# A sparse-attention layer's setup: two of four chunks done in pieces inside the loop, query scratch laid out by tile

## The chip, the cores and the metric

One core of one Trainium2 chip. The metric is the device time of one execution in microseconds, the median of several. The kernel is a whole stack of eight layers in fp32 (some products split into two rounded halves), written with explicit queues and semaphores.

## The reference

`x` is 2048 tokens of 128 features. Eight layers follow each other, each `x = x + layer(norm(x))`: gated linear attention, a four-product FFN, a state-space layer, the same FFN, the top-k attention, an integer FFN, linear attention, the integer FFN. The change is in the top-k attention. Cut to what matters:

```python
c_kv = x @ W_dkv                                  # 32 latents a token
q_i = (x @ idx_wq).reshape(B, L, 4, 64); k_i = x @ idx_wk
I = einsum('bths,h->bts', relu(einsum('bthd,bsd->bths', q_i, k_i)), idx_w)
I = where(local, inf, I); I = where(causal, -inf, I)   # window of 64, causal
_, idx = top_k(I, 96)                             # 64 of the window, 32 picked
c_q = x @ W_dq                                    # 64
query_c = c_q @ W_uq; query_r = pope(c_q @ W_qr, angles_q)   # softplus, rotated
key_r = pope((x @ W_kr)[idx], angles_k)           # rotated by rank of the pick
scores = (query_c . (c_kv @ W_uk)[idx] + query_r . key_r) * scale
out = softmax(scores) @ (c_kv @ W_uv)[idx] @ W_out
```

The kernel merges W_uq with W_uk and W_uv with W_out, so a key is one row of 96 numbers (64 for the rotary part, 32 latents) in a table in DRAM.

## The kernel before

Tokens lie along the free axis, in 4 chunks of 512 or 16 tiles of 128. A tile has 8 groups of 16 queries, 128 groups in all. PSUM has 8 banks of 512 columns.

**Setup (`topk_setup`, one version for each engine), before any attention.** When the fourth layer is done, SP loads four weights and all rope tables. PE merges the weights by 32 small matmuls (four banks, copied out by ACT at L1228 to L1230). Then for each of 4 chunks: `front` (latent query, keys, rotary queries; softplus as Abs, Exp, Ln on ACT, max and add on DVE at L1652 to L1656), `index` and `back` (four index queries and one index key, each rounded by ACT at L1250 and its rest kept by DVE at L1669; latent queries; keys turned into rows). DVE rotates the queries for the window (`rotate`, L1678 to L1680), POOL those for the picks (L558 to L560). SP stores queries, latents and key rows in DRAM. Tiles 0 and 1 are scored and picked in this stage (`EARLY = 2`).

**The loop (`topk`).** It is unrolled over slots, the same for all engines; slot s has attention step n = s - ATTN_LAG, here s - 7. Each engine has a fixed order in a slot:

- PE: `rows_turn(n+1)` (L891), `scores(n)`, `values(n-2)`, the scores of index units in `SLOT_STEPS[s]`, `probs_turn(n-1)` (L911, L912), and at a tile's end `out_project`, and `index_turn`.
- ACT: `rows_copy(n+1)` (L1303), `probs_norm(n-1)` (L1314), `out_copy(n-2)` (L1329), queries regrouped, rectified index scores (L1286), `probs_copy(n-1)`, `probs(n)` (L1309).
- DVE: `rows_rotate(n+2)` (L1748), `sum_invert(n-1)` (L1766), the addition to x, mask and picks (L1725, L1727, L1729) that come first, `row_max(n)` (L1758), then sums (L1713, L1716) and the other picks. A pick round finds 8 maxima, their places, and drops them, each over all columns of the tile; four rounds. The "rows" step (L1737) puts the finished list where POOL reads it.
- POOL: `gather(i)`: 32 indirect DMAs a tile (16 for tile 0), 4 a group, into one of two buffers. It waits for the list of tile i, and for each group for `values` of the same group of tile i-2.
- SP: for each tile 10 loads of queries (four rotary parts and one latent part, for window and picks) and 8 of values, one a group.

`SLOT_STEPS` spreads sums and picks of tiles 2 to 15 over slots 0 to 117 in proportion to a cost (columns plus 60); the list of a tile is ready a slot after its "turn". So the last, tile 15, is in slot 118. The attention of tile i covers slots 8i+7 to 8i+14.

## Time and profile before

| | us |
|---|---|
| median of 3 runs | 1364.27 |
| lowest, highest | 1357.66, 1373.55 |
| profiled execution, its span | 1540.3 |
| before the top-k setup | 450 |
| setup | 127 |
| loop | 807 |
| three layers behind | 156 |

The profiled execution has no time of its own beside its span from the first to the last instruction. In the views, a group of instructions is named by line, engine, operation and tiles; many helpers share a line (L579 is every matmul made by `mm`). PE's durations are modelled, some of its records can be missing, and "remote" or "issue" as the end of a wait means that no recorded event was found for it.

### The profile page before, as it was taken

The numbers are of one execution on the slowest core, as the hardware profiler recorded it, in microseconds if no ns is written. First come the engines' busy times: TensorE is split into PE (matmuls) and PEld (weight loads), VectorE is DVE, ScalarE is ACT, GpSimd is POOL, SyncE is SP. The second block draws the span as 40 slices with busy tenths as digits, with TensorE's granted clock in tenths as the row PEclk, the third lists the DMA queues.
The fourth block names the chain that finished last, engine by engine and source line by source line (L and its number), as shares of the span: only waits on it lengthen the run. The fifth ranks groups of instructions, "written<-read, shape, count | busy, mean of one in ns | idle before, by whom it ended". The sixth has DMA issues, their size and how long they took to land. (4 is left out here: it accounts for less than half of the span.)

```text
span 1540.3 us, 20077 instructions
## 1 busy us (share of the span) xinstructions
PE 1138.3 (74%) x6808; PEld 807.1 (52%) x6808; DVE 835.0 (54%) x1764; ACT 737.4 (48%) x1795; POOL 532.3 (35%) x532
## 2 busy tenths in 40 slices
PE   6499989979996782777677866777667636388996
PEld 2288756726671221555555645565555525375554
DVE  3477555345534564765565565665666635125436
ACT  3822367718755441554444444454545524265325
POOL 2000000000002386466666666666766463400000
PEclk7699899959985665766666677666767756577889
DMA  5000000000022143133223221322212222100000
GB/s 187 1 1 1 1 1 0 1 0 1 0 74 91 64 126 71 43 56 54 51 39 55 55 58 33 57 55 55 56 35 57 44 52 48 27 15 14 1 1 28
DMA packets 74488, 61.99 MB, mean 40 GB/s; under 512 B 31570, under 2 KB 59028, under 8 KB 73876
## 3 DMA queue, kind: packets, MB, share of 16 engines
q1 hardware_dynamic: 58516, 36.31, 9.7%
q0 software_dynamic: 15872, 24.41, 7.6%
q8 instruction: 55, 0.90, 0.2%
q14 instruction: 45, 0.37, 0.1%
HBM read 52.53 MB, written 8.13 MB: 39 GB/s over the span
## 5 line engine op out<-in xcount | busy, mean ns | idle before, releaser
L545 POOL DMA_INDIRECT arena_lo<-key_table,idx_T x496 | 490.9, 990 | 302.0 <-issue 133.9
L579 PE MATMUL bank<-arena_lo 128*32 128x32 f32 (+6 forms) x1656 | 209.8, 276 | 112.1 <-issue 55.0
L579 PEld LDWEIGHTS bank<-arena_lo 128*32 128x32 f32 (+5 forms) x1656 | 178.0, 166 | 165.7 <-issue 128.6
L558 POOL TENSOR_TENSOR arena_lo<-arena_lo 128x512 f32<-128x512 f32 x8 | 11.8, 1474 | 474.2 <-DVE arena_lo L1656 473.9
L1303 ACT ACTIVATE arena_hi<-bank 96x512 f32<-96x512 f32 x128 | 74.7, 584 | 120.3 <-remote 71.7
L1329 ACT ACTIVATE arena_hi<-bank 32x128 f32<-32x128 f32 x128 | 33.6, 262 | 200.3 <-remote 166.3
L891 PE MATMUL bank<-ident,arena_hi 128*96 128x128 f32 x512 | 111.2, 359 | 22.8 <-DVE arena_hi L1748 22.8
L1716 DVE SCALAR_TENSOR_TENSOR arena_lo<-arena_lo,iw 128x512 f32<-128x512 f32 (+4 forms) x114 | 76.0, 667 | 84.5 <-ACT arena_lo L1286 54.3
L579 PE MATMUL bank<-index_k_hi,index_q 128*128 128x512 f32 (+5 forms) x160 | 92.0, 576 | 21.0 <-ACT arena_lo L1286 11.4
L1286 ACT ACTIVATE arena_lo<-bank 128x512 f32<-128x512 f32 (+4 forms) x152 | 76.0, 510 | 56.3 <-remote 26.6
L911 PE MATMUL bank<-ident,arena_hi 128*128 128x128 f32 x128 | 48.8, 381 | 65.9 <-ACT arena_hi L1314 50.5
L891 PEld LDWEIGHTS bank<-ident,arena_hi 128*96 128x96 f32 x512 | 80.6, 168 | 31.1 <-DVE arena_hi L1748 24.2
L1758 DVE CUSTOM_DVE_ANT_0 arena_hi<-bank,score_mask 128x208 f32<-128x208 f32 x124 | 46.4, 374 | 90.2 <-issue 60.8
L579 PE MATMUL bank<-arena_hi,arena_lo 32*128 32x128 f32 x256 | 57.6, 411 | 49.2 <-ACT arena_hi L1329 48.1
L579 PEld LDWEIGHTS bank<-arena_hi,arena_lo 32*128 32x128 f32 x256 | 53.0, 311 | 54.1 <-ACT arena_hi L1329 50.8
L1725 DVE MAX8 arena_lo<-arena_lo 128x8 f32<-128x320 f32 (+13 forms) x56 | 75.6, 1350 | 0.7
L579 PE MATMUL bank<-index_k_lo,index_q 128*128 128x512 f32 (+5 forms) x160 | 75.9, 476 | 0.0
L1727 DVE FIND_INDEX8 idx_u<-arena_lo 128x8 uint32<-128x320 f32 (+13 forms) x56 | 75.7, 1351 | 0.0
L911 PEld LDWEIGHTS bank<-ident,arena_hi 128*128 128x128 f32 x128 | 22.3, 175 | 92.8 <-ACT arena_hi L1314 66.9
L579 PE MATMUL bank<-arena_hi 96*32 96x128 f32 x1024 | 70.9, 361 | 0.0
L1748 DVE TENSOR_TENSOR arena_hi<-arena_lo,rank_rope 128x384 f32<-128x384 f32 x128 | 70.7, 552 | 0.3 <-issue 0.3
L1314 ACT ACTIVATE arena_hi<-arena_hi 128x208 f32<-128x208 f32 x128 | 59.1, 462 | 13.6 <-DVE arena_hi L1766 5.9
(257 smaller groups left out, 2463.0 us busy)
## 6 DMA issues: line engine op xcount, KB each, us to landing
arena_lo<-key_table,idx_T POOLq DMA_INDIRECT x496
arena_lo<-q_l SPq DMA_DIRECT2D x64, 64.0 KB
arena_lo<-q_lat SPq DMA_DIRECT2D x32, 128.0 KB
arena_lo<-q_g SPq DMA_DIRECT2D x64, 64.0 KB
h<-in_h SPq DMA_DIRECT2D x2, 1024.0 KB, 7.8
q_l<-arena_hi SPq DMA_DIRECT2D x8, 256.0 KB
q_g<-arena_hi SPq DMA_DIRECT2D x8, 256.0 KB
q_lat<-arena_hi SPq DMA_DIRECT2D x8, 256.0 KB
```

Of the source, the lines that this page charges most:

```text
L545: pool.indirect_dma_start(out=G[b][:, q, :], out_offset=None, in_=key_table[0:index_width(i), :], in_offset=bass.IndirectOffsetOnAxis(ap=i ...
L579: return pe.matmul(out_, lhsT, rhs, start=start, stop=stop, **kw)
L891: last = pe.transpose(bank[2 + n % 2][0:ROW, j * P:(j + 1) * P], GR[n % 2][:, j, :], ident[:])
L911: pe.transpose(score_bank(n)[:, 0:P], Pr[n % 2][:, 0:P], ident[:])
L1286: fn(relu_[:, u % 4, 0:w], bank[6 + u % 2][:, 0:w], ACT.Relu).then_inc(i_relu, 1)
L1303: fn(GT[n % 2], bank[2 + n % 2][0:ROW, :], ACT.Copy).then_inc(a_gts, 1)
L1314: fn(Pr[n % 2], Pr[n % 2], ACT.Copy, scale=rsum[:, n % 2:n % 2 + 1]).then_inc(a_pn, 1)
L1716: ins = v.scalar_tensor_tensor(s_, r_, iw[:, h:h + 1], s_, ALU.mult, ALU.add)
L1725: steps.did(v.max(best, sc))
L1727: steps.did(v.max_index(idx_u[:, 8 * k:8 * k + 8], best, sc))
L1748: v.tensor_tensor(GR[n % 2], G[i % 2][:, 4 * g:4 * g + 4, :], rank_rope[:].unsqueeze(1).to_broadcast([P, 4, ROW]), ALU.mult).then_inc(a_ro ...
L1758: steps.did(v.tensor_tensor_reduce(out=Sm[b], in0=score_bank(n)[:, 0:KEYS], in1=mask[:], scale=1.0, scalar=LOWEST, op0=ALU.add, op1=ALU.ma ...
```

## The change

- The setup is cut into 12 pieces a chunk (`PIECES`): index key, four index queries, latent query, keys, two rotary queries, rows, two latent queries. A piece is one product of PE (`piece`), a copy of ACT, Exp and Ln for three of them, and an end on DVE (`piece_end`) for eight.
- `topk_front` replaces `topk_setup` and the second half of the norm before it: chunks 0 and 1 with a ring of four banks, between them the norm's steps and the picks of tiles 0 and 1. Chunks 2 and 3 go into the loop: a piece a slot from slot 5 and from slot 30 in banks 3 and 5, and then four slots with a quarter of the query rotation each (`queries_rotate`, three instructions).
- All queries are rotated by DVE; POOL only gathers, and starts when the first chunk's rows are stored.
- The weights are merged before the state layer (`merge_weights`); their loads start when the FFN's weights have been rounded.
- Rotary tables and key tables are loaded by chunk into one buffer each; index queries are kept for two chunks.
- Scratch for queries is laid out by tile, so that a tile's queries are 6 loads with runs of 4 KB on the DRAM side, and its values 2 loads instead of 8.
- ATTN_LAG 7 becomes 4, PICK_SLOTS 118 becomes 115. `rows_turn` uses one bank instead of two; turned lists lie in bank 7 with the odd index units; projected outputs in the score bank of the tile's last group.

```diff
+        q_rot = {n: dram("q_" + n, (NT, DR, NH, P)) for n in ("l", "g")}
+        q_lat = dram("q_lat", (NT, DC, NH, P))
...
+        def window_rows(i, g0, g1):
+            s0 = max(i * P + g0 * GQ - LW, 0)
+            step = GQ * ROW if i * P + g0 * GQ >= LW else 0
+            return bass.AP(key_table.tensor, s0 * ROW + 2 * DR, [[ROW, WIN], [step, g1 - g0], [1, DC]])
...
-        ATTN_LAG = NG - 1
-        PICK_SLOTS = NG * NT - 10
+        ATTN_LAG = 4
+        PICK_SLOTS = NG * NT - 13
...
+        PIECES = ("ik", "iq0", "iq1", "iq2", "iq3", "cq", "raw", "qp0", "qp1", "rows", "ql0", "ql1")
+        NPIECE = len(PIECES)
+        PIECE_SLOT = {2: 5, 3: 30}
+        def piece_bank(c, k):
+            return bank[(NPIECE * c + k) % 4] if c < FRONT else bank[(3, 5)[k % 2]]
...
+        def pieces_at(s):
+            return [(c, s - s0) for c, s0 in PIECE_SLOT.items() if 0 <= s - s0 < NPIECE]
...
+        def turns_at(s):
+            return [(c, s - s0 - NPIECE) for c, s0 in PIECE_SLOT.items() if 0 <= s - s0 - NPIECE < 4]
...
+        start, per_slot = 1, (cost(sum(SUMS[FRONT + 1:] + PICKS[FRONT:], []))) / (PICK_SLOTS - 1)
...
+            sp.wait_ge(f_w, 5)
             for n, dst in (("WuqT", WuqT), ("WukT", WukT), ("WuvT", WuvT), ("Wout", Wout)):
                 sp.dma_start(dst, d[n]).then_inc(t_w, 16)
...
+            def load_tables(c):
+                if c:
+                    sp.wait_ge(t_rot, 4 * c)
                 for k, n in enumerate(("cos_ql", "sin_ql", "cos_qg", "sin_qg")):
...
+                    sp.dma_start(rope_tab[:, k, :], d[n][:, c * C:(c + 1) * C]).then_inc(t_tab[c], 16)
...
+            def load_queries(i):
...
                     sp.wait_ge(a_q, 4 * i)
-                half = DR // 2
                 for dst, n in ((QL_in, "l"), (QG_in, "g")):
-                    for r in range(4):
-                        src = q_rot[n][r % 2][:, i * P:(i + 1) * P].rearrange("(h f) t -> f h t", f=half)
-                        sp.dma_start(dst[r * half:(r + 1) * half], src).then_inc(q_loaded, 16)
-                    src = q_lat[:, i * P:(i + 1) * P].rearrange("(h c) t -> c h t", c=DC)
-                    sp.dma_start(dst[2 * DR:ROW], src).then_inc(q_loaded, 16)
+                    for r in range(2):
+                        sp.dma_start(dst[r * DR:(r + 1) * DR], q_rot[n][i]).then_inc(q_loaded, 16)
+                    sp.dma_start(dst[2 * DR:ROW], q_lat[i]).then_inc(q_loaded, 16)
...
+            def load_values(i):
...
                 if i >= 2:
                     sp.wait_ge(a_pv, NG * (i - 1))
-                for g in range(NG):
-                    s0 = max(i * P + g * GQ - LW, 0)
-                    sp.dma_start(Vloc[b][:, g, :], key_table[s0:s0 + WIN, 2 * DR:ROW]).then_inc(v_loaded[b], 16)
+                for g0, g1 in ((0, LW // GQ), (LW // GQ, NG)):
+                    sp.dma_start(Vloc[b][:, g0:g1, :], window_rows(i, g0, g1)).then_inc(v_loaded[b], 16)
...
+            load_key_rope(1)
+            store_queries(0, 0)
+            store_queries(0, 1)
+            store_latents(0)
+            load_tables(1)
+            load_queries(0)
+            load_values(0)
...
+            for s in range(SLOTS):
+                for c, k in pieces_at(s - 1):
+                    if PIECES[k] == "rows":
+                        store_rows(c)
+                    elif PIECES[k] == "ql1":
+                        store_latents(c)
+                    elif PIECES[k] == "qp0" and c + 1 < NCH:
+                        load_key_rope(c + 1)
+                for c, half in turns_at(s - 1):
+                    if half % 2 == 1:
+                        store_queries(c, half // 2)
+                    if half == 3 and c + 1 < NCH:
+                        load_tables(c + 1)
+                i, at_ = divmod(s - ATTN_LAG, NG)
+                if at_ == 0 and 0 <= i < NT - 1:
+                    load_queries(i + 1)
+                if at_ == 2 and 1 <= i < NT - 1:
+                    load_values(i + 1)
...
-            pool.wait_ge(x_ready, 4 * L_TOPK + 4)
-            for c in range(NCH):
-                pool.wait_ge(t_mu, c + 2)
-                pool.wait_ge(t_tab[c], 80)
-                pool.wait_ge(t_store_g, STORES_Q * (c + 1))
-                cos, sin = rope_tab[c][:, 2, :], rope_tab[c][:, 3, :]
-                for b, (f0, f1, op) in enumerate(((cos, sin, ALU.subtract), (sin, cos, ALU.add))):
-                    steps.did(pool.tensor_tensor(rot_tg[:, 0, :], mu[c % 2][:, 0, :], f0, ALU.mult))
-                    steps.did(pool.tensor_tensor(rot_tg[:, 1, :], mu[c % 2][:, 1, :], f1, ALU.mult))
-                    last = pool.tensor_tensor(rot[:, 2 + b, :], rot_tg[:, 0, :], rot_tg[:, 1, :], op)
...
+            for i in range(NT):
+                if i % 4 == 0:
+                    pool.wait_ge(t_store_k, STORES_K * (i * P // C + 1))
                 gather(i)
...
@@ -771,6 +855,7 @@
             def ssm():
                 pe.wait_ge(s_ssm, N_SSM)
+                merge_weights()
                 with pe.Fori(0, NCH) as c:
...
                 for h in range(NH):
-                    last = mm(bank[0][0:DCQ, h * DC:(h + 1) * DC], WuqT[:, h, :], WukT[:, h, :])
+                    last = mm(bank[4][0:DCQ, h * DC:(h + 1) * DC], WuqT[:, h, :], WukT[:, h, :])
                 for h in range(NH):
-                    last = mm(bank[1 + h // 4][0:DC, (h % 4) * P:(h % 4 + 1) * P], WuvT[:, h, :], Wout[:, h, :])
+                    last = mm(bank[2 + h // 4][0:DC, (h % 4) * P:(h % 4 + 1) * P], WuvT[:, h, :], Wout[:, h, :])
                 last.then_inc(t_wm, 1)
...
+            def piece(c, k):
+                name, o_, tokens = PIECES[k], piece_bank(c, k), xn[:, c * C:(c + 1) * C]
+                if c < FRONT:
+                    if NPIECE * c + k >= 4:
+                        bank_released(*divmod(NPIECE * c + k - 4, NPIECE))
+                elif k >= 2:
+                    bank_released(c, k - 2)
+                elif c > FRONT:
+                    bank_released(c - 1, NPIECE - 2 + k)
...
+            def topk_front():
+                pe.wait_ge(s_tk, N_TK)
+                pe.wait_ge(x_ready, 4 * L_TOPK + 4)
+                ln_center(L_TOPK, 1)
+                for k in range(4):
+                    piece(0, k)
+                ln_mean(L_TOPK, 1)
+                for k in range(4, 7):
+                    piece(0, k)
+                ln_spread(L_TOPK, 1)
+                pe.wait_ge(ln_applied, LN0 + 4 * L_TOPK + 4)
+                sums(0)
+                for k in range(7, 10):
+                    piece(0, k)
+                index_turn(0)
+                sums(1)
+                for k in range(10, NPIECE):
+                    piece(0, k)
+                for k in range(5):
+                    piece(1, k)
+                index_turn(1)
+                for k in range(5, NPIECE):
+                    piece(1, k)
...
             def rows_turn(n):
                 pe.wait_ge(a_rot, n + 1)
-                if n >= 2:
-                    pe.wait_ge(a_gts, n - 1)
+                if n >= 1:
+                    pe.wait_ge(a_gts, n)
                 for j in range(4):
-                    last = pe.transpose(bank[2 + n % 2][0:ROW, j * P:(j + 1) * P], GR[n % 2][:, j, :], ident[:])
+                    last = pe.transpose(bank[2][0:ROW, j * P:(j + 1) * P], GR[n % 2][:, j, :], ident[:])
                 last.then_inc(a_gt, 1)
...
+                if n % (4 * NG) == 0:
+                    pe.wait_ge(t_kl, i * P // C + 1)
                 if n >= 3:
                     pe.wait_ge(a_otc, n - 2)
+                    if (n - 3) % NG == NG - 1:
+                        pe.wait_ge(a_x, (n - 3) // NG + 1)
...
-                bank5_free((a_x, i + 1))
                 for h in range(NH):
-                    last = mm(bank[5][:, 128:256], Muv[:, h, :], OT[i % 2][:, h, :], h == 0, h == NH - 1,
+                    last = mm(score_bank(NG * i + NG - 1)[:, 3 * P:4 * P], Muv[:, h, :], OT[i % 2][:, h, :], h == 0, h == NH - 1,
...
                             index_scores(i, k)
+                    for c, k in pieces_at(s):
+                        piece(c, k)
                     if 0 <= n - 1 < GROUPS:
                         probs_turn(n - 1)
                     if 0 <= n - 2 < GROUPS and (n - 2) % NG == NG - 1:
...
+            def piece_exp(c, k):
+                if softplus_of(c, k):
+                    a = softplus_of(c, k)[0]
+                    steps.did(fn(a, a, ACT.Exp, scale=-1.0))
...
+            def piece_log(c, k):
+                if softplus_of(c, k):
+                    a = softplus_of(c, k)[0]
+                    n = a.shape[0]
+                    fn(a, a, ACT.Ln, bias=one_col[0:n]).then_inc(t_ln, 1)
...
+            def topk_front():
+                ln_square(L_TOPK, 1)
+                for k in range(4):
+                    piece(0, k)
+                ln_sqrt(L_TOPK, 1)
+                act.preload_act_table_set("natural_log_exp_and_others")
+                for k in range(4, 7):
+                    whole_piece(0, k)
+                sums(0)
+                for k in range(7, 10):
+                    whole_piece(0, k)
+                sums(1)
+                for k in range(10, NPIECE):
+                    whole_piece(0, k)
+                for k in range(NPIECE):
+                    whole_piece(1, k)
...
-                fn(GT[n % 2], bank[2 + n % 2][0:ROW, :], ACT.Copy).then_inc(a_gts, 1)
+                fn(GT[n % 2], bank[2][0:ROW, :], ACT.Copy).then_inc(a_gts, 1)
...
+                    for c, k in pieces_at(s):
+                        piece(c, k)
                     if 0 <= n - 1 < GROUPS:
                         probs_copy(n - 1)
+                    for c, k in pieces_at(s):
+                        piece_exp(c, k)
                     if 0 <= n < GROUPS:
                         probs(n)
+                    for c, k in pieces_at(s):
+                        piece_log(c, k)
+                act.wait_ge(t_store_l, STORES_L * NCH)
+                steps.leave(steps.k, 1)
...
+            def piece_end(c, k):
+                name, o_ = PIECES[k], piece_bank(c, k)
+                at_, ring = slice(c * C, (c + 1) * C), slice(c % 2 * C, c % 2 * C + C)
+                if name == "ik":
+                    dve.wait_ge(t_iqh, 5 * c + k + 1)
+                    v.tensor_tensor(k_lo[:, at_], o_, k_hi[:, at_], ALU.subtract).then_inc(t_iqs, 1)
+                elif name[:2] == "iq":
+                    q = q_split[int(name[2])][64:P, ring]
+                    dve.wait_ge(t_iqh, 5 * c + k + 1)
+                    v.tensor_tensor(q, o_[64:P, :], q, ALU.subtract).then_inc(t_iqs, 1)
+                elif name == "raw":
+                    dve.wait_ge(t_ln, 3 * c + 1)
+                    v.scalar_tensor_tensor(raw[0:2 * DR, :], o_[0:2 * DR, :], 0.0, raw[0:2 * DR, :], ALU.max, ALU.add)\
+                        .then_inc(t_rawd, 1)
...
+            def queries_rotate(c, half):
+                which, b = divmod(half, 2)
+                cos, sin = rope_tab[:, 2 * which, :], rope_tab[:, 2 * which + 1, :]
+                f0, f1, op = ((cos, sin, ALU.subtract), (sin, cos, ALU.add))[b]
+                if half == 0:
+                    dve.wait_ge(t_mu, 2 * c + 2)
+                    dve.wait_ge(t_tab[c], 64)
+                if c == 0 and half == 0:
+                    dve.wait_ge(ln_inv, 4 * L_TOPK + 4)
+                if c >= 1 and b == 0:
+                    dve.wait_ge((t_store_q, t_store_g)[which], STORES_Q * c)
+                v.tensor_tensor(rot_tmp[:, 0, :], mu[:, 0, :], f0, ALU.mult)
+                steps.did(v.tensor_tensor(rot_tmp[:, 1, :], mu[:, 1, :], f1, ALU.mult))
+                v.tensor_tensor(rot[:, half, :], rot_tmp[:, 0, :], rot_tmp[:, 1, :], op).then_inc(t_rot, 1)
+                dve.wait_ge(t_rot, 4 * c + half + 1)
+            def topk_front():
...
+                for k in range(2):
+                    piece_end(0, k)
+                ln_invert(L_TOPK, 1)
+                for k in range(2, 5):
+                    piece_end(0, k)
+                ln_apply(L_TOPK, 1)
+                piece_end(0, 6)
+                for step, _ in SUMS[0] + PICKS[0][:-1]:
+                    pick(*step)
+                piece_end(0, 7)
+                pick(0, "rows", 0)
+                keys_rotate(0)
+                piece_end(0, 8)
+                for step, _ in SUMS[1] + PICKS[1][:-1]:
+                    pick(*step)
+                for half in range(2):
+                    queries_rotate(0, half)
+                for k in range(4):
+                    piece_end(1, k)
+                pick(1, "rows", 0)
+                for half in range(2, 4):
+                    queries_rotate(0, half)
+                for k in range(4, 7):
+                    piece_end(1, k)
+                keys_rotate(1)
+                for k in (7, 8):
+                    piece_end(1, k)
+                for half in range(4):
+                    queries_rotate(1, half)
...
+                    for c, k in piece_ends_at(s):
+                        piece_end(c, k)
+                        if PIECES[k] == "qp0":
+                            keys_rotate(c)
+                    for c, half in turns_at(s):
+                        queries_rotate(c, half)
```

## Rows read from the trace of the kernel before

**Rows 1.** Windows by stage: start:end, length, busy (instructions) by engine, clock, DMA share, GB/s.

```profile
450.00:577.00 127.00, 91.90 (x194) 36.37 (x194) 68.03 (x124) 57.44 (x90) 56.38 (x47) 0.61 0.36 106
577.00:616.00 39.00, 8.06 (x33) 4.54 (x31) 15.75 (x41) 7.13 (x17) 24.41 (x26) 0.59 0.35 74
616.00:1292.00 676.00, 471.87 (x3466) 366.23 (x3464) 417.33 (x977) 322.50 (x1028) 413.01 (x416) 0.67 0.25 49
1292.00:1384.00 92.00, 54.35 (x504) 46.22 (x504) 19.11 (x85) 36.67 (x133) 30.59 (x32) 0.65 0.13 28
1384.00:1540.30 156.30, 130.09 (x456) 77.78 (x454) 75.27 (x133) 68.49 (x128) 0.00 (x0) 0.86 0.04 14
```

**Rows 2.** POOL's gathers: group of instructions, one line's instructions, timeline.

```profile
L545 POOL DMA_INDIRECT arena_lo<-key_table,idx_T x496 | 490.9, 990 | 302.0 <-issue 133.9 <-remote 71.2 <-PE bank L579 59.1
...
L545 POOL DMA_INDIRECT arena_lo<-key_table,idx_T x496: 942/947/1475, 539.1 to 1334.8; - x166
...
1292.11 0.95 POOL L545 DMA_INDIRECT arena_lo<-key_table,idx_T  x1 [18.55 <-DVE idx_T L1737]
```

**Rows 3.** Timeline of ACT behind the last picks: start, duration, engine, line, operation.

```profile
1369.17 0.58 ACT L1303 ACTIVATE arena_hi<-bank 96x512 f32<-96x512 f32 x1
1371.42 0.59 ACT L1303 ACTIVATE arena_hi<-bank 96x512 f32<-96x512 f32 x1
```

**Rows 4.** Groups of instructions, 616 to 1292: busy, mean ns, idle before them.

```profile
L1725 DVE MAX8 arena_lo<-arena_lo 128x8 f32<-128x576 f32 (+12 forms) x50 | 72.4, 1448 | 0.6
L1716 DVE SCALAR_TENSOR_TENSOR arena_lo<-arena_lo,iw 128x512 f32<-128x512 f32 (+4 forms) x107 | 71.5, 668 | 80.5 <-ACT arena_lo L1286 54.3 <-issue 23.7
...
L1758 DVE CUSTOM_DVE_ANT_0 arena_hi<-bank,score_mask 128x208 f32<-128x208 f32 x107 | 40.0, 374 | 72.0 <-issue 60.8 <-remote 6.9 <-DVE idx_u L1727 0.9
...
L911 PEld LDWEIGHTS bank<-ident,arena_hi 128*128 128x128 f32 x110 | 19.5, 178 | 82.3 <-ACT arena_hi L1314 60.7 <-issue 18.2
L1766 DVE RECIPROCAL arena_hi<-arena_hi 128x1 f32<-128x1 f32 x111 | 17.4, 157 | 28.9 <-ACT arena_hi L1309 23.4 <-issue 4.3
```

**Rows 5.** Stalls: ACT's waits (us, count, longest), and the timeline around two.

```profile
ACT arena_hi L1329 <- remote: 166.3, 46, 25.0
...
914.60 0.27 PE L912 MATMUL bank<-ident,arena_hi 128*80 128x128 f32 x1
919.26 0.27 ACT L1329 ACTIVATE arena_hi<-bank 32x128 f32<-32x128 f32 x1 [4.87 <-remote]
...
611.09 0.19 DVE L1737 CAST idx_T<-bank 128x32 uint32<-128x32 f32 x1 [17.88 <-remote]
```

**Rows 6.** Timeline: the weights' 32 products, and the state layer's start.

```profile
458.47 5.46 PE L579 MATMUL bank<-arena_lo 64*64 64x32 f32 x32
...
312.38 1.87 PE L579 MATMUL bank<-xn,sBT 128*64 x2
...
314.75 1.27 DVE L1632 TENSOR_TENSOR_SCAN ssm_state_sb<-ssm_keep,ssm_carry,bank 64x512 f32 x1 [0.34 <-DVE ssm_carry L1627]
```

**Rows 7.** Timeline: the loop's first sum.

```profile
577.70 0.39 DVE L1713 TENSOR_SCALAR arena_lo<-arena_lo,iw 128x320 f32<-128x320 f32 x1 [3.14 <-issue]
```

**Rows 8.** Groups of instructions, 450 to 577.

```profile
L579 PE MATMUL bank<-xn,Wiq 128*128 128x512 f32 x32 | 22.4, 865 | 0.0
...
L1250 ACT ACTIVATE index_q<-bank 128x512 fp32r<-128x512 f32 x16 | 8.4, 584 | 4.4 <-PE bank L579 3.8 <-issue 0.6
...
L1244 ACT ACT_TABLE_LOAD x4 | 5.1, 1283 | 0.1
...
L1725 DVE MAX8 ln_sq<-ln_sq 128x8 f32<-128x96 f32 (+1 forms) x8 | 2.5, 311 | 0.3
```

**Rows 9.** Timeline of DVE's rotations, and a gather of POOL beside them.

```profile
485.67 1.64 DVE L1679 TENSOR_TENSOR arena_lo<-arena_lo 128x512 f32<-128x512 f32 x1
...
548.14 1.15 POOL L545 DMA_INDIRECT arena_lo<-key_table,idx_T  x1 [0.30 <-issue]
548.51 0.69 DVE L1679 TENSOR_TENSOR arena_lo<-arena_lo 128x512 f32<-128x512 f32 x1
```

533 lines of the change are left out of this document (242 added, 291 removed).

## The prediction

> **What bounds the kernel now.** I read the windows by stage first. The span falls into 450 us before the top-k layer, 127 us of setup up to the first step of the big loop, 39 us of lead-in, 676 us of attention beside picks, 92 us of attention after the last picks, and 156 us of tail [rows 1]. The reader should see that no engine is full in the loop: of 676 us PE is busy 472, DVE 417, POOL 413, ACT 323, at a mean granted clock of 0.67, so most of it at the lower level, 1.2 GHz.
>
> Next, who waits for whom. POOL issues one gather each 1.25 us (0.95 of work at the median and 0.30 of issue [rows 2, 9]); four gathers make a group, so POOL needs 5.0 us a group, 40 us a tile, and it waits: gather(i, g) may start only when values(i-2, g) is done. 59.1 us of its waits are put down to PE. Before the 32 gathers of tile 15 it waits 18.55 us for that tile's index list, and then they run from 1292.1 without waiting but once, the last from 1334.8 [rows 2]. The loop ends 48 us after the last of them, since a long stall of this execution had held the attention back; undisturbed, the end of the loop is the list of tile 15, plus 40 us of gathers, plus some 12 for the last one's landing and five slots, which without picks take 2.25 us each [rows 3]. So what sets the end is the moment when DVE has made the last list (slot 118, step n = 111). Before that, a slot is a round trip between four engines in fixed orders: PE waits 82.3 us in 110 slots for the normed probabilities before it turns them (0.75 us a slot), and DVE waits 72.0, 80.5 and 28.9 us for scores, rectified sums and exponents, 181 us in 111 slots or 1.6 us a slot [rows 4].
>
> **The profiled execution against the median.** It took 1540.3 us, the median is 1364.3, 176 us less. ACT's wait for the values at L1329 alone is 166.3 us here [rows 5], in 46 pieces up to 25.0 us. In one of them PE's last recorded work before its gap ends at 914.9 and what its earlier matmuls release starts at 919.3; another holds DVE for 17.88 us before tile 2's list (L1737) [rows 5]. I take these stalls for the difference, so all differences below are added to 1364.3; I can't show it. Checked: 1364.3 - 450 - 127.7 - 20 (lead-in without that stall) - 52 - 156.3 leaves 558 us for 111 slots, 5.0 us a slot.
>
> **Part 1, weights merged earlier: +5 us (4 to 6).** The 32 small matmuls (5.46 us) move from setup to PE's queue between the last norm spread and the state layer's first matmul. There PE starts at 312.38 and the scan follows 0.34 us late at 314.75 [rows 6]: no cover. The scan would start at 312.4 + 5.5 + 1.9 = 319.8, 5.1 us later. Copies on ACT lie in its idle time.
>
> **Part 2, setup for two chunks instead of four: -57 us (-43 to -68).** Before: 450.0 to DVE's first sum at 577.70, 127.7 us [rows 7]. After, by engine from the same rows. PE: a chunk is 5 index projections, keys, latent query, two rotary and two latent queries, eleven products of two passes at 0.865 us or a little more [rows 8], and four turns: 21 us; two chunks 42, the norm about 6, the scores of tiles 0 and 1 about 6: 54 us, the lower bound with 5 us of fill. DVE, which ends last: norm and first splits until 472; tile 0's sums and picks 7 (11 instructions of three kinds like L1725 at 0.31 us [rows 8], the rest sums) to 480; key rotation and two halves of softplus 2; tile 1's sums and picks 7.5 to 491; now all four quarters of chunk 0's rotation, 12 instructions of 0.69, 8.3 us; nine splits and softplus ends of chunk 1, 6.2. That is 505 to 508. Then chunk 1's rotation needs tables that SP loads only after chunk 0's rotation (502) and two waits behind stores: landed at about 512.7. 12 x 0.69 more ends at 521. Upper bound: another 14 us if the one ring of four banks and picks in DVE's order hold PE up.
>
> The rotations of the picked queries move from POOL to DVE. In the trace a rotation on DVE takes 1.64 us while POOL rotates too and 0.69 while POOL issues gathers [rows 9]; I take 0.69 throughout. The Trainium skill (GPSIMD Engine Reference, 1. Specifications) says the two engines share SBUF interfaces and contend where a DVE instruction has two SBUF inputs. If that held for POOL's gathers too, 48 rotations would cost 0.95 us more each, 46 us in all; the row at 548.51 beside a gather speaks against it. POOL's gathers no longer wait for POOL's rotations; gather(0) can start at about 484 instead of 539, but its rows are needed only at step 0, so nothing comes of it.
>
> Of ACT, the table loads of 1.283 us, one for Exp and one for Ln in each of 4 chunks [rows 8], should go, since one set is loaded ahead. ACT isn't last in my sum, so no gain is booked.
>
> **Part 3, lead-in: -1.5 us.** The lag falls from 7 slots to 4, the picks end at slot 115, again step 111. Spread by the kernel's own costs, 36 sums and picks lie in slots 0 to 6 before, and 24 in slots 0 to 3 after. At 320 to 448 columns I take 0.55 and 0.5 us each, between the mean of the front (0.31, 96 and 192 columns [rows 8]) and that of the loop (1.45, over 400 to 1984 columns [rows 4]): 19.7 and 12.2 us. So step 0 comes 7.5 us earlier relative to the loop's start, but the same picks must then be done in the same 111 steps: 7.5 us of DVE work moves there. DVE has 1.6 us of waits a slot; four fifths of it, 6 us, I book (0 to 8).
>
> **Part 4, two chunks in pieces inside the loop: +32 us (0 to 80).** 24 slots get a piece: on PE two passes (1.73 us) between the sums and the turn of the probabilities, on ACT one to three instructions of 0.6, on DVE one or two of 0.69. Eight slots get a quarter of a chunk's rotation, three instructions, 2.1 us of DVE. Behind PE's piece stand probs_turn, ACT's copy, the exponent, and DVE's reciprocal. PE had 0.75 us of wait just there, so 1.0 us of 1.73 stays: 24 us. Six pieces have Exp and Ln (1.2 us) before and after probs: half, 4 us. Rotations against 1.6 us of DVE waits: 0.5 x 8 = 4. From below nothing, if POOL's 5.0 us a group or the round trip hides all; from above all of it in row, 24 x (1.73 + 0.58) + 7.6 + 17 = 80 (0.58 ACT's copy, L1250 [rows 8]). I take 32, nearer to the lower end, since every engine shows idle time [rows 1].
>
> **Part 5, layout and loads: -6 us (-35 to 0).** A tile's queries are 10 loads, 768 KB in 512-byte pieces, and 8 loads of values; now 6 and 2. They are issued four slots ahead, and ACT waits nowhere for them, so the loads as such bring nothing. But the stall at 914.9 lies where such a load is issued. Were 2.5 us of each of 14 tile changes due to it, 35 us would go; I can't see that outside this profile and take 6. The stores write the same bytes.
>
> **Part 6, shared banks: +3 us (0 to 10).** Turned rows have one bank, lists share a bank with odd sums, projected outputs lie in a score bank. Behind PE's new waits stand scores. DVE's add comes while PE turns rows (1 us), so the wait is mostly covered; 0.2 us a tile.
>
> Sum: 5 - 57 - 1.5 + 32 - 6 + 3 = -24.5 us. 1364.3 - 24.5 = 1339.8, so 1340 (the profiled execution: about 1516). Tail and the 52 us after the last list stay.
>
> **Rivals.**
> A, the pieces are hidden: POOL's 5.0 us a group equals the pace of 5.0. If the attention really follows POOL, or fuller engines are granted more clock, part 4 costs nothing: 1308. For it: idle time on all engines, and PE's passes shorten wherever the full clock is granted. Against: POOL waits for values in the trace, not the reverse. 0.20.
> B, slower: the round trip takes each piece at full length at 1.2 GHz. Part 4 is 80, the time 1388. It becomes slower than before when 32 slots cost over 56.5 us, 1.8 us each. For it: PE busy 70% at the low clock and DVE 62% leave little in a slot of 5. 0.15.
> C, the front gains less or ACT changes tables in the loop. Six Exp-Ln pieces with two loads of 1.283 us are 15.4 us; 15 us of waits in the front do the same: 1355. 0.18. The Trainium skill (ScalarE: Activation LUTs, Table sets) says that natural_log_exp_and_others holds both functions, which speaks for no such loads; no row of before shows that set kept, since each Exp and each Ln has its load.
> D, the change doesn't do what it says: too small to count beside C, for the setup is really two chunks shorter.
>
> **How the numbers follow.** The forecast has 0.47, its own range 1325 to 1355. All cases to eight in ten: 1306 to 1380, which leaves out part of B and little of A. A measurement can tell about 1% from no change, here 1350.6 and 1377.9. Faster: 0.40 of the forecast's 0.47 and all of A, 0.60. Same: the forecast's other 0.07 and C's 0.18, 0.25. Slower: B's 0.15.
>
> **What would show it.** The scan about 5 us later; the first sum of the loop about 71 + 5 us after the norm instead of 127.7; 24 slots longer by 1 us; no table load inside the loop; the last list about 24 us earlier, with 52 us from there to the norm in an undisturbed run. I am wrong if DVE or PE in slots 5 to 20 and 30 to 45 takes over 1.8 us more, if POOL waits for nothing (then A), or if new stalls end at q loads.

## The result

The changed kernel took 1300.1 us (median of 4 runs, 1286.6 to 1303.4) against 1361.0 us before: a ratio of 0.9546 with a 95% interval from 0.9502 to 0.9591, 61 us less. The forecast was 1340, the lower end of its range 1306.

The chips that the runs came to are of two kinds: one runs the kernel before in 1351 to 1374 us and the other in 1525 to 1559 us, and the profile of before that the prediction rests on (1540.3 us) is of the other kind than its median (1364.3 us). A second run of the changed kernel on a chip of the first kind gave 0.9486 (0.9419 to 0.9553, 1290.8 us), one on a chip of the second kind 0.9535 (0.9485 to 0.9585, 1484.7 against 1549.5 us). Below, "gapless" chips are the first kind, for POOL's gathers have no gaps there, and "stalling" chips the second. Each chip was used at one time only, so that the difference lies in the chip and not in the occasion is taken for granted, not shown. Unless a chip is named, a number is of the gapless kind.

The windows by stage of the changed kernel (start:end, length, then busy us with the number of instructions of PE, weight loads, DVE, ACT and POOL, granted clock, DMA share, GB/s), which answer to [rows 1]:

```profile
450.00:512.60 62.60, 44.29 (x125) 20.40 (x123) 43.20 (x100) 33.55 (x64) 29.16 (x29) 0.76 0.46 109
512.60:1119.00 606.40, 484.09 (x3953) 376.77 (x3952) 470.48 (x1129) 375.15 (x1184) 461.58 (x468) 0.75 0.30 72
1119.00:1146.00 27.00, 21.85 (x110) 16.14 (x111) 4.57 (x19) 10.61 (x31) 0.07 (x1) 0.50 0.12 41
1146.00:1301.60 155.60, 129.57 (x435) 77.14 (x433) 73.75 (x129) 64.52 (x121) 0.00 (x0) 0.84 0.02 7
```

The setup is 62.6 us long instead of 127, the tail is as before. Now POOL's gathers in the same trace, the group and then the timeline, answering to [rows 2]:

```profile
L648 POOL DMA_INDIRECT gathered_rows<-key_table,idx_T x496 | 490.8, 990 | 592.8 <-DMA key_table<-key_rows 439.4 <-issue 147.5 <-PE bank L663 5.8
```

```profile
474.91 1.09 POOL L648 DMA_INDIRECT gathered_rows<-key_table,idx_T  x1 [439.44 <-DMA key_table<-key_rows]
...
1049.35 0.17 DVE L1891 CAST idx_T<-bank 128x32 uint32<-128x32 f32 x1
...
1077.95 0.94 POOL L648 DMA_INDIRECT gathered_rows<-key_table,idx_T  x1 [0.30 <-issue]
...
1118.13 0.94 POOL L648 DMA_INDIRECT gathered_rows<-key_table,idx_T  x1 [0.30 <-issue]
```

The reader is to see that POOL, over the whole kernel the engine with the fewest busy us (38% of the span), hardly stops from 474.91 to 1119.07: 490.8 us of gathers, 147.5 us of issue between them, and 5.8 us of waiting for PE. The list of tile 15 (L1891) is ready at 1049.35, and its first gather starts at 1077.95, with 0.30 us of issue ahead of it as everywhere: the list lay ready for 28 us before POOL came to it. Behind the last gather's end there are 182.5 us. That is the theory that the experiments test, called G: **the row of 496 gathers sets the time; what counts is when the first starts, not when anything else is done.** The prediction's own reading, that DVE's last list sets the end, is called L.

### The profile page after: what moved, and what is told of

It is laid out like the page before. It is cut to its first block and busy times, and to the rows that moved or that the text cites. A ratio compares the mean times of both kernels' runs of the same rounds, so it can differ in the third digit from the quotient of the medians.

```text
span 1301.6 us, 19937 instructions
## 1 busy us (share of the span) xinstructions
PE 1067.0 (82%) x6808; PEld 771.8 (59%) x6808; DVE 828.7 (64%) x1780; ACT 730.5 (56%) x1803; POOL 498.5 (38%) x508
## 5 line engine op out<-in xcount | busy, mean ns | idle before, releaser
L648 POOL DMA_INDIRECT gathered_rows<-key_table,idx_T x496 | 490.8, 990 | 592.8 <-DMA key_table<-key_rows 439.4
L1902 DVE TENSOR_TENSOR rotated_rows<-gathered_rows,rank_rope 128x384 f32<-128x384 f32 x128 | 71.5, 558 | 75.0 <-DMA gathered_rows<-key_table,idx_T 74.5
L985 PE MATMUL bank<-ident,rotated_rows 128*96 128x128 f32 x512 | 104.1, 341 | 4.6 <-DVE rotated_rows L1902 4.6
L1437 ACT ACTIVATE turned_rows<-bank 96x512 f32<-96x512 f32 x128 | 74.3, 581 | 44.3 <-PE bank L985 44.2
L1420 ACT ACTIVATE index_relu<-bank 128x512 f32<-128x512 f32 (+5 forms) x160 | 76.8, 496 | 24.2 <-PE bank L663 21.8
L1870 DVE SCALAR_TENSOR_TENSOR index_sums<-index_relu,iw,index_sums 128x512 f32<-128x512 f32 (+5 forms) x120 | 77.6, 647 | 19.6 <-ACT index_relu L1420 15.3
L985 PEld LDWEIGHTS bank<-ident,rotated_rows 128*96 128x96 f32 x512 | 75.2, 159 | 12.2 <-DVE rotated_rows L1902 5.6
L1879 DVE MAX8 top<-index_sums 128x8 f32<-128x96 f32 (+15 forms) x64 | 78.2, 1222 | 1.3
L1881 DVE FIND_INDEX8 idx_u<-top,index_sums 128x8 uint32<-128x96 f32 (+15 forms) x64 | 78.1, 1220 | 0.0
L663 PE MATMUL bank<-turned_rows,q_picked 96*32 96x128 f32 x1024 | 66.0, 338 | 0.0
L1883 DVE MATCH_REPLACE8 index_sums<-top,index_sums 128x96 f32<-128x96 f32 (+15 forms) x48 | 58.1, 1210 | 0.0
```

The costliest lines, as they stand in the source:

```text
L648: pool.indirect_dma_start(out=G[b][:, q, :], out_offset=None, in_=key_table[0:index_width(i), :], in_offset=bass.IndirectOffsetOnAxis(ap=i ...
L663: return pe.matmul(out_, lhsT, rhs, start=start, stop=stop, **kw)
L985: last = pe.transpose(bank[2][0:ROW, j * P:(j + 1) * P], GR[n % 2][:, j, :], ident[:])
L1420: fn(relu[:, u % 4, 0:w], bank[6 + u % 2][:, 0:w], ACT.Relu).then_inc(i_relu, 1)
L1437: fn(GT[n % 2], bank[2][0:ROW, :], ACT.Copy).then_inc(a_gts, 1)
L1870: ins = v.scalar_tensor_tensor(s_, r_, iw[:, h:h + 1], s_, ALU.mult, ALU.add)
```

## The experiments

### The kernel before, profiled on other chips (e1, e7, e14)

No edit.

> The kernel before, unchanged, profiled once more. Theory G (the gathers on POOL set the end in both kernels: the time is the first gather's start plus an unbroken row of 496 gathers at about 1.30 us plus 182.5 us behind the last one, as in the trace of the changed kernel): if this execution is free of the long stalls, its span is near 1361, the gathers run from about 539 to about 1180 us with no gap over 0.35 us inside a tile from tile 2 on, and every list is ready well ahead of its gathers. Theory L (of the prediction: DVE's last list sets the end): the list of tile 15 is ready about 92 us before the norm behind the loop, and POOL waits for it and for the lists before it.

> The kernel before, profiled again. Theory G, on a chip that runs it in about 1361 us: first gather at about 539 us, one break of some 8.6 us for POOL's rotation of chunk 3, then tiles 2 to 15 without a gap over 0.35 us, the last gather's end near 1180 and 182 us behind it. Theory L: POOL waits for lists or values for over 30 us in tiles 2 to 15 also there.

> The kernel before, profiled. On a chip that runs it in about 1361 us, theory G: the first gather at about 536 us, a break of 8.6 us for POOL's rotation of chunk 3 and one for the list of tile 2, then no gap over 0.35 us inside a tile from tile 3 on, the last gather's end near 1178 and 182 us behind it, and list 15 at least 20 us ahead of its first gather. Theory L: list 15 is ready about 92 us ahead of the loop's end and POOL waits for it.

e1 (1538.4 us) and e7 (1559.0 us) came to stalling chips and look like the profile ahead of the prediction. e14 came to a gapless one: 1371.0 us, span 1369.2. Its gathers and their surroundings, in order of time:

```profile
539.23 1.13 POOL L545 DMA_INDIRECT arena_lo<-key_table,idx_T  x1 [4.49 <-DMA key_table<-arena_hi]
...
559.60 1.29 POOL L558 TENSOR_TENSOR arena_lo<-arena_lo 128x512 f32<-128x512 f32 x1
...
568.20 1.13 POOL L545 DMA_INDIRECT arena_lo<-key_table,idx_T  x1 [0.27 <-POOL arena_hi L560]
...
1119.78 0.17 DVE L1737 CAST idx_T<-bank 128x32 uint32<-128x32 f32 x1
...
1148.55 0.94 POOL L545 DMA_INDIRECT arena_lo<-key_table,idx_T  x1 [0.30 <-issue]
...
1187.27 0.94 POOL L545 DMA_INDIRECT arena_lo<-key_table,idx_T  x1 [0.31 <-issue]
```

and two lines of its waits (us in total, times, longest):

```profile
POOL arena_lo L545 <- issue: 145.7, 478, 0.3
...
DVE arena_hi L1748 <- DMA arena_lo<-key_table,idx_T: 121.7, 63, 5.0
```

So the kernel before was bound by the same row. Its list 15 is ready 28.8 us before POOL comes to it; from tile 3 on POOL waits for no list and no values; instead DVE waits 121.7 us for gathered rows, where it waited for scores, sums and exponents in [rows 4]. Only two things break the row: POOL's rotations of chunk 3 (559.6 to 568.2) and 2.5 us ahead of tile 2, together 10.5 us more than the issue time that would stand there anyway. The two profiles, before (e14) against after, then give the whole gain in three terms:

| us | before | after | |
|---|---|---|---|
| first gather starts | 539.2 | 474.9 | -64.3 |
| from there to the last one's end | 649.0 | 644.2 | -4.8 |
| behind it | 181.0 | 182.5 | +1.5 |
| span | 1369.2 | 1301.6 | -67.6 |

67.6 us between two profiled executions, 61 between the medians. The row lost e14's two breaks, 10.5 us, but only 4.8 are left of that: in the trace of after the gathers take 990 ns on average instead of 983, and POOL waits 5.8 us for PE.

### The first gather held back (e2, e6, e12)

```diff
+            pool.wait_ge(t_rot, 8)
             for i in range(NT):
                 if i % 4 == 0:
                     pool.wait_ge(t_store_k, STORES_K * (i * P // C + 1))
                 gather(i)
```

> The changed kernel, but POOL waits with its first gather until DVE has rotated the queries of chunk 1 (512.6 us in the trace of after instead of 474.9). Nothing else is late by that: the first gathered rows are needed at step 4. Theory G: the whole row of gathers moves by 37.7 us, less some 3 us because fewer gathers lie beside the rotations: 1300 + 35 to 38 = 1335 to 1338. Theory L and the round trip of the engines: 0 to 2 us, for the lists are made as before.

> The changed kernel with the first gather held back until the rotations of chunk 1 are done, again, beside the changed kernel itself. Theory G (the row of gathers sets the end), where the chip runs the gathers without a gap: 35 to 38 us over e5. Theory L (DVE's last list sets it): 0 to 2 us. Where POOL waits for values in the trace, both expect 0 to 10 us.

> The changed kernel with the first gather held back until the rotations of chunk 1 are done (37.7 us), a third time. On a chip where the gathers run without a gap (before in about 1361 us), theory G: 35 to 38 us over the changed kernel, a ratio to before of 0.976 to 0.980; theory L, by DVE's last list: 0 to 2 us, 0.951 to 0.956. On the other kind of chip as in e6, 0.978.

e12 ran on a gapless chip: 1326.7 us, 0.9751 of before (0.9683 to 0.9819), against 0.9546 and 0.9486 of the changed kernel on two others, so 28 to 36 us slower. e16 below, whose time can't be told from the changed kernel's, ran on the same chip as e12 and took 35.3 us less. G had 35 to 38, L 0 to 2. The rows:

```profile
504.00 1.10 POOL L648 DMA_INDIRECT gathered_rows<-key_table,idx_T  x1 [469.77 <-DVE rotated L1820]
...
511.62 0.59 ACT L1438 ACTIVATE turned_rows<-bank 96x512 f32<-96x512 f32 x1 [5.10 <-PE bank L986]
...
1072.64 0.17 DVE L1892 CAST idx_T<-bank 128x32 uint32<-128x32 f32 x1
...
1101.11 0.94 POOL L648 DMA_INDIRECT gathered_rows<-key_table,idx_T  x1 [0.30 <-issue]
...
1139.82 0.95 POOL L648 DMA_INDIRECT gathered_rows<-key_table,idx_T  x1 [0.30 <-issue]
```

The rotations were done at 503.9 here and not at 512.6, so that the first gather is 29 us later than in the traces of after (474.9) and e11 (474.2), not the 37.7 that I had reckoned with. From the first gather to the end are 818.0 us here, 826.7 in the trace of after, 817.1 in e11's, and 830.0 in e14's, of which 10.5 are its two breaks. The loop began 9 us earlier than in the trace of after, and the attention's first rows were copied at 511.6 instead of 520.5; yet the end came 20 us later than in that trace, 31 us later than in e11's. The list of tile 15 came 23 us later too (1072.6 against 1049.4), since DVE waits for gathered rows in its slots, and even so lay ready for 28 us. So the gathers pace the lists, not the lists the gathers, and L falls here.

e6 stands beside the changed kernel on one stalling chip: 1518.3 against 1484.7 us, 33.6 more. Its first gather was 38.4 us later (516.35 against 477.99). e2 (0.9781 of before) agrees. I had expected at most 10 where POOL waits. So a late first gather costs nearly its delay there too, although the row has gaps; why is the last part of this section.

### The changed kernel again (e5, e11)

No edit; the ratios stand in the result.

> The changed kernel, unchanged, as the base of this call. The chip of the last call ran the kernel before in 1550 us, the chip of the result in 1361. On a chip of the first kind: as in the result, 0.955 of before, gathers without a gap. On one of the second kind (there PE's signals come late in bursts while gathers run, and POOL waits for values in both kernels): the change's shorter setup of 57 us, its pieces and loads give 0.96 to 0.98 of before.

> The changed kernel, unchanged, as the base of this call: 0.953 to 0.955 of before by both kinds of chip so far.

### The pieces in the loop (e3, e9, e13)

e9 lets PE compute a quarter of each piece's columns; e3 and e13 do PE's product of each piece, ACT's copy of 20 of the 24 and DVE's rotations twice. The cores of both edits (e9's ahead of the dots, e3's and e13's behind them):

```diff
-                name, o_, tokens = PIECES[k], piece_bank(c, k), xn[:, c * C:(c + 1) * C]
+                n_ = C if c < FRONT else C // 4
+                name, o_, tokens = PIECES[k], piece_bank(c, k)[:, 0:n_], xn[:, c * C:c * C + n_]
...
+                for again in range(2 if c >= FRONT else 1):
...
+                    if c >= FRONT:
+                        steps.did(fn(k_hi[:, at_], o_, ACT.Copy))
                     fn(k_hi[:, at_], o_, ACT.Copy).then_inc(t_iqh, 1)
```

> The changed kernel, but PE computes only the first 128 of the 512 columns of each piece in the loop (the rest of the bank keeps older numbers, so the last two chunks' keys and queries are mostly wrong; ACT, DVE and the transfers do all of their work). It takes 24 x 1.3 us, less four turns, off PE. Theory L with the prediction's price: 15 to 20 us faster than e11. Theory G, where gathers run without a gap: 0 to 2 us.

> The changed kernel with the work of the 24 pieces in the loop done twice: PE's product of two passes (or the four turns), ACT's copy for 20 of them, and the three rotation instructions of each of the 8 quarters on DVE. The prediction's price of the pieces (PE's 1.0 us of 1.73 each, rotations 0.5 us each) would add about 30 us, its upper bound 80 us. Theory G: 0 to 5 us, for PE and DVE have the room beside 5.2 us of gathers a group.

> The changed kernel with the work of the 24 pieces in the loop done twice, as in e3. On a chip where the gathers run without a gap (before in about 1361 us): theory G 0 to 8 us over the changed kernel, for the pieces lie in slots 5 to 45, where POOL's lead over the attention is up to a tile; the prediction's price would be 30 us. On the other kind of chip as in e3: 27 to 35 us, 0.976 of before.

e9: 1295.7 us against 1290.8 of e11 on the same chip, no gain (0.9495 against 0.9486), though PE's products and turns for the pieces took 17.5 us instead of 32.8. PE's busy time from 512 to 1119 us fell by less, from 485.2 to 480.9; the granted clock was 0.73 there instead of 0.75. In both traces the rows of attention step 8 are copied 37.5 us after those of step 0, a stretch with pieces in it. So PE's part of the pieces lies in the shadow of the gathers and costs nothing that can be measured. ACT's and DVE's parts weren't taken away in any run; for them speaks that POOL waits only 5.8 us for PE, and for no list, in the whole row of after, so that little of them can have reached it.

e3 and e13 both came to stalling chips: 1510.8 us (0.9761) and 1498.0 us (0.978). Against the changed kernel on a third such chip (0.9535, 1484.7 us) that is 35 and 38 us by the ratios, 26 and 13 us by the times; the prediction had charged 32 for one copy. So by the ratios its price holds on these chips, and G's 0 to 5 us don't; but no run of the changed kernel itself stands beside either on the same chip. Doubling wasn't tried on a gapless chip.

### The loads (e8, e17)

The old loads again, ten of queries and eight of values a tile; the scratch also gets a gap behind every 512 bytes, so that the queries come in pieces of that size.

```diff
-                    for r in range(2):
-                        sp.dma_start(dst[r * DR:(r + 1) * DR], q_rot[n][i]).then_inc(q_loaded, 16)
+                    for r in range(4):
+                        h0, half = r % 2 * (DR // 2), DR // 2
+                        sp.dma_start(dst[r * half:(r + 1) * half], q_rot[n][i][h0:h0 + half]).then_inc(q_loaded, 16)
...
-                for g0, g1 in ((0, LW // GQ), (LW // GQ, NG)):
+                for g in range(NG):
```

> The changed kernel with the old loads: ten loads of queries and eight of values a tile, queries in pieces of 512 bytes (the scratch has a gap behind every 512 bytes). The prediction's term: 6 us slower than e11 (0 to 35). Theory G, where gathers run without a gap: 0 to 3 us. Theory S (on a chip where PE's signals come late, the gathers hold PE off, not the loads): 0 to 6 us. A rival there (the loads hold PE off): 20 to 35 us.

> The changed kernel with the old loads, as in e8. Where the gathers run without a gap: as in e8, 0 to 5 us, 0.949 to 0.957 of before. On the other kind of chip: if the loads hold PE off there, 20 to 35 us over the changed kernel, 0.966 to 0.977; if not, up to 6 us, 0.953 to 0.958.

e8: 1295.4 against 1290.8 us on the same chip (0.9516, 0.9452 to 0.9581, against 0.9486): no difference that can be told. e17, on a stalling chip: 0.971 (0.9648 to 0.9773), which is 27 us over the changed kernel by the ratios, but 4 us by the times themselves (1488.3 against 1484.7), since that chip ran the kernel before in 1537 instead of 1549 us. What the loads cost there, 4 or 27 us, stays open.

### The lists earlier (e10, e19)

All lists are due up to eight slots earlier, and the pieces move with them.

```diff
-        PICK_SLOTS = NG * NT - 13
+        PICK_SLOTS = NG * NT - 21
-        PIECE_SLOT = {2: 5, 3: 30}
+        PIECE_SLOT = {2: 4, 3: 27}
```

> The changed kernel with PICK_SLOTS 107 instead of 115, and the pieces from slots 4 and 27: all lists are ready up to eight slots earlier, and the slots before have 7% more picks. In the trace of e5 POOL waits 16 and 19 us for the lists of tiles 14 and 15, in the trace of after not at all. Theory L, there: 25 to 35 us faster than e11. Theory G, where gathers run without a gap: within 5 us of e11.

> The changed kernel with the picks done by slot 107, as in e10. Where the gathers run without a gap: as in e10, 0.962 of before. On the other kind of chip, where POOL waits 16 and 19 us for the lists of tiles 14 and 15: 25 to 35 us faster than the changed kernel, 0.930 to 0.938, if those waits are on the path; within 5 us of it if the attention behind them is.

In e10, list 15 and its first gather:

```profile
1014.73 0.17 DVE L1891 CAST idx_T<-bank 128x32 uint32<-128x32 f32 x1
...
1083.12 0.94 POOL L648 DMA_INDIRECT gathered_rows<-key_table,idx_T  x1 [0.30 <-issue]
```

This is the sharpest evidence against L: the list was ready at 1014.7 us instead of 1048.1 (e11), 33 us earlier, and the kernel took 17 us more (1307.5, 0.9618 with 0.9556 to 0.968). POOL waited some 16 us for values in tiles 2 to 4, and its row was 654.2 us long instead of 641.6. That the denser picks made the attention late there is my reading; the pieces moved too, and no run parts the two. I had expected it within 5 us: what delays the row early costs too. e19 on a stalling chip: 0.9534 (0.945 to 0.9618), the same as the changed kernel by the ratio, 23 us less by the time. List 15 came 59 us earlier than in e5 and POOL no longer waited for it, so at most a part of my 25 to 35 us was there.

### A quarter of the gathers left out (e4, e15)

```diff
                 for q in range(FIXED // QD if i == 0 else 0, P // QD):
+                    if i >= 2 and q % 4 == 3:
+                        continue
```

> The changed kernel without every fourth gather of tiles 2 to 15 (three instead of four in a group; the rows of two tiles before stay in the place of the fourth, so the attention uses other rows, but all other work is done). It takes 112 of 496 gathers, 146 us, off POOL. Theory G: the time falls until the next bound; DVE with 470 of 606 us busy in the trace of after allows about 60 us, so 1240 to 1285. Theory L: the gathers behind the last list are fewer, at most 10 us: 1290 to 1300.

> The changed kernel without every fourth gather of tiles 2 to 15 (three instead of four in a group; older rows stay in the place of the fourth, all other work is done). On a chip where the gathers run without a gap, theory G: 112 gathers of 1.30 us are 146 us; DVE with 470 of 606 us busy in the trace of after, and its waits on the round trip, allow 40 to 90 of it: 0.89 to 0.93 of before. Theory L: at most 10 us less than the changed kernel. On the other kind of chip as in e4, 0.875.

e15: 1233.7 us, 0.9043 (0.8974 to 0.9113), 60 to 68 us less than the changed kernel by the ratios, where 146 us of POOL's work are gone. Two waits of its profiled execution (1250.7 us, the longest of the four) between 512 and 1060 us show what follows:

```profile
POOL gathered_rows L650 <- PE bank L665: 73.9, 32, 8.2
...
POOL gathered_rows L650 <- DVE idx_T L1893: 21.5, 2, 14.5
```

Now POOL waits for PE's values and even for lists; DVE is busy 468 of 550 us. The next bound lies 60 us or a little more below the row of gathers, and that is the room in which the pieces are free. e4 on a stalling chip: 1357.1 us, 0.8745, or 122 to 128 us less. 112 gathers fewer, so 1.1 us for each, though POOL waited there.

### The rotation's factors read from PSUM (e16)

```diff
+                    if s == PIECE_SLOT[3] + NPIECE:
+                        fn(bank[5][:, 0:ROW], rank_rope[:], ACT.Copy).then_inc(rope_moved, 1)
...
+                moved = n + ATTN_LAG - 2 >= PIECE_SLOT[3] + NPIECE + 2
+                factors = bank[5][:, 0:ROW] if moved else rank_rope[:]
```

> The changed kernel, but from slot 44 on DVE's product that rotates the gathered rows reads its factors from PSUM (ACT copies them into bank 5 behind the last piece), so that two thirds of these 128 instructions have one SBUF input instead of two. If these inputs hold POOL up, the gathers beside them keep to 0.94 us: the mean over 496 falls from 0.99 to 0.97 to 0.975, the row of gathers is 7 to 10 us shorter, the time 5 to 10 us less than the changed kernel. If not, both stay within 2 us.

The group of gathers between 720 and 1060 us, first of the changed kernel (e11):

```profile
L648 POOL DMA_INDIRECT gathered_rows<-key_table,idx_T x264 | 261.0, 989 | 80.5 <-issue 79.5 <-PE bank L663 0.9
```

and of e16:

```profile
L648 POOL DMA_INDIRECT gathered_rows<-key_table,idx_T x267 | 259.5, 972 | 81.4 <-issue 79.3 <-PE bank L663 2.1
```

989 ns become 972. Taken apart by what DVE does beside them, gathers that overlap a rotation by over 0.2 us and no sum fall from 1.04 to 0.96 us, and those beside neither are 0.95 us in both. The mechanism is there, but it is worth 4.5 us in this stretch, half of what I expected; the row was 640.9 us against 641.6, and the time (1291.4 us, 0.9496 with 0.9426 to 0.9565) can't be told from e11.

### The stalling chips

In e2, PE's last values product before a stall, then two instructions that wait for PE, of DVE for scores and of ACT for the values:

```profile
1204.06 0.64 PE L664 MATMUL bank<-probs_picked,gathered_rows 128*32 128x32 f32 x8
...
1212.89 0.38 DVE L1913 CUSTOM_DVE_ANT_0 masked_scores<-bank,score_mask 128x208 f32<-128x208 f32 x1 [6.48 <-issue]
...
1228.92 0.27 ACT L1464 ACTIVATE attn_out<-bank 32x128 f32<-32x128 f32 x1 [24.06 <-remote]
```

The product is recorded until 1204.7, the copy that waits for it starts 24 us later. All the while POOL gathers without a pause; it stops at 1225.0, and 4 us later PE's results are there. The stalls [rows 5] are of this form: the one of 17.88 us ended at 611.1, two us behind the end of a tile's gathers at 609.1, and of ACT's 15 waits of over 4 us at L1329 between 640 and 1210 us in the profile of before each ended 1.05 to 1.62 us after POOL had stopped, which by then waited for values itself. It isn't strict: DVE got its scores at 1212.9, while POOL gathered. On gapless chips the same gathers, even denser, hold nobody up. I conclude that on stalling chips a gather beside the loop costs about 1.1 us (e4) and one beside the setup little: e6's 38.4 us later start moved some 30 gathers from the one place to the other, for 33.6 us. In e6 the rows of attention step 2 were copied 40.7 us behind those of step 1, at 576.3, just as the gathers of tile 1 ended (576.6); in e5, where these had ended at 540.2, the same step took 4.4 us. That PE's results come late on these chips while gathers run is what these times say; by what mechanism, and why only there, stays open.

## Why the prediction was wrong

**What sets the end: wrong, and the cause of the rest.** "So what sets the end is the moment when DVE has made the last list" holds in the trace it was read from, where POOL waits 18.55 us for that list [rows 2], not in the executions of which the median was to be forecast. The profile was 176 us above the median, and I took the difference for stalls on top of an otherwise right picture; in truth the stalls had turned a bound engine into a waiting one. The numbers to see it were in hand: 496 gathers of 0.99 + 0.30 us are 640 us; from 539 us with 8.6 us of rotations they end at 1188, and 12 + 156 us behind them make 1356, within 1% of the median. (The 12 us were too few: from the last gather's end to the norm it is 25 us in e14 and 27 in after, which would make 1369, also within 1%.) Also the check that I did, 558 us for 111 slots or 5.0 us, was POOL's own 5.0 us a group. I wrote the equality into rival A and gave it 0.20, "for POOL waits for values in the trace".

**"gather(0) can start at about 484 instead of 539, but its rows are needed only at step 0, so nothing comes of it": the step that failed.** It started at 474.9, and that is 64 us of a gain of 61 (medians) to 68 us (profiles); e12 takes 29 us of it back and loses 28 to 36. The rotations of picked queries, moved off POOL, freed another 8.3 us of the row, which the sum didn't have either; the row came out 4.8 us shorter.

**Part 1, +5 us: right in the trace of after, too much in e11's.** In the trace of after:

```profile
307.26 1.91 PE L663 MATMUL bank<-WukT,WuqT 64*64 64x32 f32 x16
309.10 3.62 PE L663 MATMUL bank<-Wout,WuvT 64*32 64x128 f32 x16
...
314.78 1.27 DVE L1767 TENSOR_TENSOR_SCAN ssm_state_sb<-ssm_keep,ssm_carry,bank 64x512 f32 x1 [5.49 <-PE bank L663]
```

The scan follows the norm's spread (303.54) by 11.2 us, in e14 by 6.1. In e11 the same products took 3.0 us instead of 5.5, and the scan was 1.4 us late: the granted clock from 303 to 316 us was 0.87 there and 0.50 in after.

**Part 2, setup: right in kind, 10 us too long.** The loop's first sum:

```profile
504.41 0.69 DVE L1817 TENSOR_TENSOR ln_diag<-mu,rope_tables 128x512 f32<-128x512 f32 x1 [5.88 <-DMA rope_tables<-in_sin_qg]
...
512.62 0.39 DVE L1867 TENSOR_SCALAR index_sums<-index_relu,iw 128x320 f32<-128x320 f32 x1
```

It comes 61 us after the FFN's end (451.8) instead of 71; before it was 128. So the term of -57 measured -67, within its range. The late tables are there as foreseen, but at 504.4 instead of 512.7, since DVE was through with the norm and the first splits 5 us earlier and with tile 0's picks in 5.7 instead of 7 us. In e12 the loop began at 503.8, earlier still, and the end came later. The table loads went as said: one at L1402 (459.67), none in the loop, so rival C falls.

**The rotations and POOL.** I weighed whether DVE's rotation is slower beside a gather, found 0.69 us and dropped it. The other side of the same row [rows 9] was the telling one: the gather took 1.15 us. The rule of the Trainium skill (GPSIMD Engine Reference, 1. Specifications), that the two share SBUF interfaces and contend where a DVE instruction has two SBUF inputs, holds here for gathers, and it is POOL that pays: 1.04 us beside a rotation, 0.95 us beside none (e11), and 0.96 beside one when one input was moved to PSUM (e16).

**Parts 3 to 6: no term on the path.** The pieces' +32 us (0 to 80) were about 0 on the chips of the result, its lower bound, as far as PE's part goes (e9), and 13 to 38 us for a second copy on stalling ones (e3, e13). "PE had 0.75 us of wait just there" is no less on a gapless chip: in e14 the same weight loads (L911) wait 139.0 us between 616 and 1188 us, against 82.3 [rows 4]. What the sum lacked is that a slot there lasts as long as its gathers. The loads' -6 us were 0 to 5 (e8). The lag and the shared banks weren't tried alone; where DVE waits 70 us for gathered rows in the loop, they may have cover. The last list came 70 us earlier (1119.8 to 1049.4), not 24, and it didn't matter; from it to the norm are 93 us in e14 and 97 in after, not 52, for it lies ready 28 us.

**The rivals.** A had the mechanism and, by a sum that was right by luck (a setup 52 us shorter with the merge in it, instead of a first gather 64 us earlier), nearly the number, 1308. B has something to it on stalling chips only. The sign and most of the chance (0.60 for faster) were right; the chance of A was too small.

## What to carry to other kernels

Before asking what a queue waits for, add up the engine that works in strict order, with its issue time, and set its row from first start to last end against the median: if it fits, an earlier start of that row is worth its full length, whatever "needs" its results when. And when the profiled execution is far from the median, a wait in it may be the disturbance and not the kernel; take the reading that also reproduces the median. Work put beside such a row is free up to the next bound, which leaving out part of the row measures (here 60 us).

## What was not expected of the hardware

- The same program takes 1361 us on some chips and 1550 on others. In the changed kernel nearly all of the difference lies in the loop (815.6 us in e5, 633.4 in after); there PE's results reach their readers up to 24 us after the product's record while gathers run, and the change is worth the same share on both (0.9546 and 0.9535).
- A gather takes 0.94 us of POOL and 0.30 us of issue; beside DVE's rotation of gathered rows, which has two SBUF inputs, it takes 1.04 us on average, up to 1.3.
